# One POOL instruction per block step: the softmax row sums of a head pair added as 2x512 columns

## The reference

```python
x = x + 0.5 * ffn(layernorm(x))            # fp4 quantize-dequantize in blocks of 16 before each product, silu(gate) * up
x = x + attn(layernorm(x))                 # 16 heads of 64; softmax over 512 keys; projection, bias, residual, layernorm
x = x + 0.5 * ffn(layernorm(x))

# attention, per head
attn = softmax(einsum('bnqd,bnkd->bnqk', q, k) * 64 ** -0.5, axis=-1)
o = einsum('bnqk,bnkd->bnqd', attn, v)
y = o @ w_proj + b_proj + x
```

## Time and profile before

| | |
|---|---|
| Median of 3 runs | 2264.16 us (2262.68 to 2269.3) |
| The profiled execution | 2263.16 us |
| Its span, first to last instruction | 2261.4 us |
| Busy: PE, PEld | 2142.7 us (95%), 1094.4 us |
| Busy: DVE, POOL, ACT | 1605.5 us (71%), 1407.7 us (62%), 1151.4 us (51%) |
| Mean granted TensorE clock | 0.978 of full speed |

### The profile page before, as it was taken

How to read it: one execution, slowest core, us unless ns; L and a number is a source line. 1 busy time by engine, 2 the same in 40 slices (tenths; PEclk the granted TensorE clock), 3 DMA queues, 4 the chain that set the end, 5 groups by cost and what they waited for, 6 DMA issues and landing times.

```text
span 2261.4 us, 38387 instructions
## 1 busy us (share of the span) xinstructions
PE 2142.7 (95%) x14537; PEld 1094.4 (48%) x14537; DVE 1605.5 (71%) x2609; ACT 1151.4 (51%) x1749; POOL 1407.7 (62%) x1289
## 2 busy tenths in 40 slices
PE   3899999999999999999999999999999999999974
PEld 2344444545445454545545454554544545454432
DVE  5565767767687786868777686877778687776634
ACT  2455554645555454555545455455555545454532
POOL 3365666757576675757756576675757667665642
PEclk8799999999999999999999999999999999999986
DMA  1000000000000000000000000000000000000000
GB/s 60 1 7 2 6 2 2 12 2 7 7 7 7 2 11 2 7 7 7 7 2 11 2 7 7 2 12 2 10 3 6 7 2 12 2 2 7 2 7 10
DMA packets 167493, 15.83 MB, mean 7 GB/s; under 512 B 148304, under 2 KB 166928, under 8 KB 167312
## 3 DMA queue, kind: packets, MB, share of 16 engines
q1 hardware_dynamic: 167312, 13.39, 5.1%
HBM read 7.03 MB, written 4.19 MB: 5 GB/s over the span
## 4 chain that ended last, share of the span: by engine, by line
PE 85%; DVE 6%; SPq 2%; issue 2%; POOL 2%; DMA 1%; ACT 1%; POOLq 0%; DVEq 0%
PE pS L934 23%; PE pO L961 20%; PE pM L918 9%; PE pX L946 5%; PE pM L1077 5%; PE pX L985 5%; PE pM L973 3%; PE LpF L333 2%; PE FpF L333 2%; SPq L568 2%; PE FpF L296 2%; PE LpF L296 2%; PE LpF L309 2%; PE FpF L309 2%; PE LpF L324 1%
## 5 line engine op out<-in xcount | busy, mean ns | idle before, releaser
L676 POOL TENSOR_TENSOR ES<-ES,E 128x512 f32<-128x512 f32 x512 | 654.9, 1300 | 217.1 <-ACT E L747 209.9
L747 ACT ACTIVATE E<-pS 128x1024 f32<-128x1024 f32 x512 | 523.2, 1022 | 459.9 <-PE pS L934 421.3
L799 DVE TENSOR_REDUCE nmax<-pX 128x2 fp32r<-128x1024 f32 x512 | 622.0, 1215 | 113.4 <-PE pX L946 98.4
L961 PE MATMUL pO<-E,VA 128*64 128x512 f32 x2048 | 552.3, 618 | 0.0
L670 POOL TENSOR_TENSOR ES<-E 128x512 f32<-128x512 f32 x256 | 321.9, 1279 | 247.5 <-ACT E L747 247.5
L918 PE MATMUL pM<-xf,w_raw 128*64 128x512 f32 x1024 | 267.1, 600 | 2.8 <-DVE QL L889 2.1
L934 PE MATMUL pS<-QH,KH 64*128 64x512 f32 x1024 | 255.9, 496 | 0.0
L946 PE MATMUL pX<-KH,QH 64*128 64x512 f32 x1024 | 241.0, 412 | 4.7 <-DVE nmax L799 3.3
L934 PEld LDWEIGHTS pS<-QH,KH 64*128 64x128 f32 x1024 | 95.5, 183 | 288.1 <-issue 269.3
L946 PEld LDWEIGHTS pX<-KH,QH 64*128 64x128 f32 x1024 | 186.3, 306 | 36.7 <-DVE nmax L799 8.0
L934 PE MATMUL pS<-SH,onesr 64*128 64x512 f32 x1024 | 203.6, 393 | 0.0
(11 more groups left out here) (178 smaller groups left out, 3000.0 us busy)
## 6 DMA issues: line engine op xcount, KB each, us to landing
RROW<-RC SPq DMA_DIRECT2D x512, 2.0 KB, 2.0
xin<-in_L_attn_x SPq DMA_DIRECT2D x16, 256.0 KB, 3.0
SH<-nmax SPq DMA_DIRECT2D x256, 2.0 KB, 2.0
LC<-LROW SPq DMA_DIRECT2D x256, 2.0 KB, 2.1
out<-X SPq DMA_DIRECT2D x16, 256.0 KB, 2.5
w_raw<-in_L_attn_w_q SPq DMA_DIRECT2D x1, 512.0 KB, 3.6
w_raw<-in_L_attn_w_k SPq DMA_DIRECT2D x1, 512.0 KB, 4.7
w_raw<-in_L_attn_w_v SPq DMA_DIRECT2D x1, 512.0 KB, 5.6
```

Source lines behind the costliest of these rows:

```text
L676: ins = g.tensor_tensor(ES[i % 3][:, hd, :], ES[i % 3][:, hd, :], E[s][:, hd, :], ALU.add)
L747: a.activation(E[s][:, :, :], pS[:, :, :], ACT.Exp).then_inc(s_exp, 1)
L799: v.tensor_reduce(nmax[px % 2][:, :, t:t + 1], pX[:, :, :], AX.X, ALU.max, negate=True).then_inc(s_max, 1)
L961: ins = pe_.matmul(pO[half(hd), :], VA[of][:, kt, j * 128 + 64 * hd:j * 128 + 64 * hd + 64], E[kt][:, hd, :], start=kt == 0, stop=kt == KT ...
```

## The change

In both places where POOL adds blocks of E, the loop over the two heads goes and one instruction takes both heads. The semaphore s_add is raised once a step as before, and the waits ahead of it are the same. A pair has three such instructions in place of six, 384 in place of 768 in all, and each has 1024 columns in place of 512. Nothing else changes: the same elements are added in the same order, and the queues of the other engines are the same.

```diff
                         if s == 1 and there(i, NP):
                             pool.wait_ge(s_exp, 4 * i + 2)
                             wait(pool, s_l, (i - 3) // 2 + 1)
-                            for hd in range(2):
-                                ins = g.tensor_tensor(ES[i % 3][:, hd, :], E[0][:, hd, :], E[1][:, hd, :], ALU.add)
-                            ins.then_inc(s_add, 1)
+                            g.tensor_tensor(ES[i % 3][:, :, :], E[0][:, :, :], E[1][:, :, :], ALU.add).then_inc(s_add, 1)
                         if s > 1 and there(i, NP):
                             pool.wait_ge(s_exp, 4 * i + s + 1)
                             pool.wait_ge(s_add, 3 * i + s - 1)
-                            for hd in range(2):
-                                ins = g.tensor_tensor(ES[i % 3][:, hd, :], ES[i % 3][:, hd, :], E[s][:, hd, :], ALU.add)
-                            ins.then_inc(s_add, 1)
+                            g.tensor_tensor(ES[i % 3][:, :, :], ES[i % 3][:, :, :], E[s][:, :, :], ALU.add).then_inc(s_add, 1)
```

## The result

The changed kernel took 2289.29 us (median of 5 runs, 2288.68 to 2289.82) against 2264.16 for the kernel before (5 runs beside it): a ratio of 1.0114 [1.0097, 1.013]. It is slower by 1.1%, where 2285 was forecast. Its profiled execution took 2289.62 us, a span of 2287.8, 26.4 us more than the span of before.

What follows compares the result with a forecast made beforehand. PE was taken to bound the kernel between start-up and tail; 13.2 + 9.8 + 3.3 + 1.1 - 6.2 - 0.4 = +20.8 us on the profiled 2263.16 gave 2284.0, and 2285 for the median; range 2262 to 2302.

Steps and rivals of the forecast that it cites:

- What the change saves: 384 fewer POOL instructions: 0.15 us less a step, 58 us of POOL in all, covered by PE's work.
- (a): L222 on Lxn, 14 times: held to the end of the wide addition, L880 late, PE waits; +13.2 us.
- (b): L161 in the norm of X1, 13 times: let go 1.08 us later, PE loses 0.74 each; +9.8 us.
- (e): L162 in the norm of Yacc, 5 times: gets in before the addition, stalls go; -6.2 us, other end +5.4.
- (f): L201 on Fh, 13 times: held longer, but L880 waits for PE's L1038 anyway; 0, bound +4 us.
- (c): Two steps back to back, three places: L161 meets the second step's first addition while PE waits; +3.3 us.
- (d): L202 in the tail, once: PE's L985 waits for the maxima behind it; +1.1 us.
- The fill: The few steps POOL itself leads at start-up; with those in the tail, forecast at -0.4 us.
- absorbed: First rival: shifted starts let L222 or L161 in ahead of the addition; 2258 to 2274 us, chance 0.20.
- turns falling worse: Second rival: L162 loses its race and L201's longer holds cost their bound; 2301, over 2300 us; chance 0.12.
- a hold that isn't tied to the length: Third rival: DVE's hold doesn't grow with POOL's instruction, only gains remain; under 2258 us, chance 0.08.
- the signs: Expected in the new profile: L222's median about 2.75 us, L161's about 2.0, L162's holds gone, PE's busy time unchanged.

Runs made afterwards that it cites:

- Eighths: Kernel before, but with eight POOL instructions of 128 columns in each adding step instead of two of 512; 2280.49 us, ratio 1.0071 to the kernel before.
- wide_26: Kernel before, but with one 1024-column instruction in step t = 26 of each batch alone, the one L222 on Lxn meets; 2282.60 us, ratio 1.0082.
- wide_18: Kernel before, but with one 1024-column instruction in step t = 18 of each batch alone, beside the norm of X1; 2273.81 us, ratio 1.0024.
- first768_26: Kernel before, but in step t = 26 alone the two instructions have 768 and 256 columns instead of 512 each; 2272.74 us, ratio 1.0053.
- wide_14: Kernel before, but with one 1024-column instruction in step t = 14 alone, the step ahead of the norm of Yacc; 2258.93 us, ratio 0.9976.
- after_third: The changed kernel run once more, unaltered, for another profile of the half-clock stretches; 2286.66 us, ratio 1.009 to the kernel before.
- quarters: Kernel before, but with four POOL instructions of 256 columns in each adding step; 2247.39 us, ratio 0.9908 to the kernel before.
- restored: Changed kernel, but with two 512-column instructions again in five of each batch's 24 adding steps (t = 5, 15, 18, 23, 26); 2253.25 us, ratio 0.9952 to before.
- norm_best: As norm_wide, but with two 512-column instructions in steps t = 5 and t = 26; 2247.71 us, ratio 0.9912 to the kernel before.
- norm_wide: Changed kernel, but the norm's L156 becomes a reduction on DVE and L161 and L162 move to POOL; 2264.26 us, ratio 0.9986 to the kernel before.

## Why the prediction was right, and where a size was off

**What the change saves.** Right: 55.8 us of POOL for 58, under PE's cover. Eighths shows where such cover ends.

**(a) and (b), the two that carry the sum.** Right to 0.1 us each in all of the 27 places, and each step alone gives its own delays at its own places (wide_26, wide_18). first768_26 gives half of (a) at an unchanged count of instructions, so it is the length of the one in the way that costs, as derived from the single case of the earlier trace rows.

**(e), the gain that hung on 0.15 us.** Right, -6.3 for -6.2, and wide_14 gives it alone. That the 0.15 us fell well in all five batches was in part luck: in wide_26 and first768_26 the same place went both ways from batch to batch at shifts as small. The wide end that I had left for it was fair.

**(f).** Right at 0 for nearly all of its places. One cost 0.4 us (near 246 us, in both profiles of the changed kernel) and one 0.15; its bound of +4 us is far off.

**(c) and (d), mis-sized.** The term that was off is the price of each: I added 1.08 us per stall and no more, 4.4 us, and they measured 8.2. The holds did grow by that (2.10 to 2.98 with a start that lies 0.15 earlier, 2.00 to 3.07), but behind three of these four places PE ran at half its clock, where in before it did so behind one. after_third gives the same sum, 8.4: 2.4 to 2.5 us at each of the three places with such a stretch, and 1.1 at the one without. How much of this the change itself brought is open, for wide_14 and wide_18 have the stretches, and lose 1.5 us by one where before has none, at stalls that didn't grow. Rows for this were at hand: before has such a stretch at 294.1, behind its own stall of 2.07 us.

**The fill, mis-sized.** -0.4 forecast, +2.1 measured. Since after_third has -0.3 with the same additions, and quarters, which starts with others, has about what after has, that difference is not the change's. I take it for chance of the single execution.

Together these two are the distance from 20.8 to 26.9. The median of after is 4.3 us over the forecast. That it isn't more is in part luck, since small gains of 0.2 to 0.3 us in a batch, which the forecast didn't have, offset some of it: the middle batch lasts 134.4 us, where 134.7 was forecast.

**The rivals.** The first, absorbed, didn't happen: no L222 or L161 got in ahead of its addition, and the distance on which it hung (0.44 us) is still 0.44 in after. The second, turns falling worse, didn't either: (e) fell well, (f) cost next to nothing. The third, a hold that isn't tied to the length, is refuted by the five lengths above. Of the signs, two were wrong. PE's busy time was to stay, and it rose by 6.2 us. L161's median was to rise to about 2.0 us, and it fell to 0.17. The working had the reason itself (a chain that met both holds now meets one), and I didn't carry it over to the median; the maximum, 2.2, was the sign to name.

**Open.** Why restored gains 0.3 to 0.4 us per batch beyond (e), of which the small waits at t = 15 and t = 27 make about half. What decides on the clock behind stalls of 2 to 3 us, and so how much of (c) and (d) is the change's. Not tried: another form for L222 that could not be held, which would leave all additions wide, and the same for L201 and L202.

## What to carry to other kernels

In this kernel DVE instructions with two inputs in SBUF, and the small `tensor_scalar` ones from SBUF to SBUF, stood still for almost as long as the one POOL instruction in their way ran, even those on four columns. The reductions, the batch-norm statistics and the instructions with one input in PSUM did not (below). So before merging POOL's instructions to save their fixed cost, look for DVE instructions far over their own minimum, and ask of each whether the bounding engine waits behind it; if a few steps do, cut the POOL work there (restored, norm_best) or give the small DVE work another form, and if POOL has room, cut everywhere (quarters: 2247.39 us, with norm_best's 2247.71 the fastest here, and both under the two kernels compared). Too fine a cut comes back as a late POOL: 1024, 512, 256 and 128 columns gave 2289.3, 2264.2, 2247.4 and 2280.5 us.

## What the runs showed of the hardware that was not expected

- Behind seven of nine stalls of PE of 2.90 to 3.08 us, and behind nine of 26 of 1.82 to 2.10 us, PE ran at 1.2 GHz for 3.4 us, twice for 6.8. A stretch of 3.4 us cost some 1.5 us (wide_14, wide_18 against before). The same stall had one in one execution and none in the next (3.07 us in after and after_third).
- The hold depends on the form of the DVE instruction. A reduction over two strided columns (128x4 from 128x8) took 161 to 165 ns in all 48 cases of norm_wide, where the two-input form of the same work took 1128 ns in the median in after. In after the low part of K (L889, one input in PSUM, one in SBUF) started in 109 of 128 cases with over 0.6 us of an addition of POOL still to run, and took 674 to 693 ns in all of them; L153's statistics (one input in SBUF) did so in 175 of 256, at 269 to 295 ns.
- POOL is held in turn: an addition of 1024 columns behind L220 took 2.65 us in place of 2.38.
- The start-up is not the same from one execution to the next: the first exp lay between 81.4 and 84.0 us after the start, a spread of 0.1% of the span, in executions whose code is the same up to there.
